# A two-layer perceiver on one core: projections on fp16 halves of fp32 values, with the lower halves of the turned tiles taken from PSUM by VectorE

## The reference, cut to what matters

```
kv = y_main @ [Wk, Wv] + bias             # context rows 256 wide, 2 x 512 columns
x  = x + attn(ln(q), ln(k), v) @ Wo + bo  # cross-attention
x  = x + selfattn(ln(x) @ Wq, ln(x) @ Wk, ln(x) @ Wv) @ Wo + bo
x  = x + ffn(x)
```

## Time and profile before

| | us |
|---|---|
| median of 3 runs | 3878.39 (3876.9 to 3882.73) |
| the profiled execution, its own time | 3881.73 |
| its span, first to last instruction | 3880.0 |
| context attention of layer 0, 16 batch elements | about 180 to 1338.6 |
| self-attention of layer 0 | 1338.6 to about 1590 |
| TensorE busy (matmul) / VectorE / ScalarE / GpSimd | 86% / 69% / 56% / 51% of the span |

### The profile page before, as it was taken

The page is one execution under the profiler, slowest core; times in us unless marked ns, Lnnn a source line. Parts: engine busy times, 40 slices in busy tenths (PEclk is TensorE's granted clock), DMA queues, the critical chain, the costliest instruction groups (busy, mean ns, idle before and its releaser), DMA issues. The chain is left out here.

```text
span 3880.0 us, 87607 instructions
## 1 busy us (share of the span) xinstructions
PE 3347.8 (86%) x34694; PEld 2418.0 (62%) x34694; DVE 2684.3 (69%) x4083; ACT 2172.2 (56%) x3767; POOL 1987.9 (51%) x2436
## 2 busy tenths in 40 slices
PE   5799999999999599548991589999999999959739
PEld 2577777777777455436770357777777777745425
DVE  5688888888888234336774478888888888816552
ACT  1367777777777422115660247777777777732231
POOL 5267767767767411232214527767767767731000
PEclk7899999999999699768995799999999999969869
DMA  2200000000000120008986110000000000030010
GB/s 78 72 29 28 29 28 21 28 30 20 29 29 11 60 51 0 32 15 285 300 269 190 23 65 28 29 25 25 29 29 20 28 30 20 11 85 0 22 65 22
DMA packets 98467, 212.45 MB, mean 55 GB/s; under 512 B 35669, under 2 KB 44629, under 8 KB 91946
## 3 DMA queue, kind: packets, MB, share of 16 engines
q1 hardware_dynamic: 89386, 181.98, 14.3%
q0 software_dynamic: 8704, 25.19, 2.3%
HBM read 174.58 MB, written 32.56 MB: 53 GB/s over the span
## 5 line engine op out<-in xcount | busy, mean ns | idle before, releaser
L265 POOL TENSOR_TENSOR a_elo<-a_e 128x1024 f16<-128x1024 f32 (+1 forms) x448 | 899.9, 2009 | 250.5 <-ACT a_e L337 241.3
L477 PE MATMUL a_ps_k<-l_wk,a_yh 128*128 128x512 f32 (+1 forms) x1664 | 625.4, 416 | 24.9 <-DVE a_yl L364 23.8
L477 PE MATMUL a_ps_v<-l_wv,a_yh 128*128 128x512 f32 (+1 forms) x1664 | 622.7, 415 | 13.7 <-DVE a_v L391 10.5
L335 ACT ACTIVATE a_e<-a_ps_t 128x1024 f32<-128x1024 f32 (+1 forms) x448 | 430.3, 961 | 143.9 <-PE a_ps_t L545 136.9
L400 DVE TENSOR_REDUCE a_mx<-a_ps_m 128x2 f32<-128x1024 f32 x384 | 466.2, 1214 | 6.8 <-PE a_ps_m L515 4.3
L246 POOL TENSOR_TENSOR a_khat<-a_kc,a_rstd 128x512 f32<-128x512 f32 (+1 forms) x416 | 449.6, 1088 | 17.5 <-PE a_ps_kt L498 7.0
L337 ACT ACTIVATE a_e<-a_ps_t 128x1024 f16<-128x1024 f32 (+1 forms) x448 | 427.5, 954 | 1.6 <-PE a_ps_o L572 1.6
L364 DVE TENSOR_TENSOR a_yl<-a_y,a_yh 128x256 fp32r<-128x256 f32 (+1 forms) x416 | 385.7, 928 | 22.4 <-ACT a_yh L293 18.5
L477 PEld LDWEIGHTS a_ps_k<-l_wk,a_yh 128*128 128x128 f32 (+1 forms) x1664 | 304.8, 183 | 143.4 <-issue 45.8
L477 PEld LDWEIGHTS a_ps_v<-l_wv,a_yh 128*128 128x128 f32 (+1 forms) x1664 | 304.2, 183 | 138.8 <-issue 57.6
L568 PE MATMUL a_ps_o<-a_v,a_e 128*128 128x65 f16 (+1 forms) x3328 | 360.0, 195 | 18.7 <-POOL a_elo L265 18.7
(11 more groups left out here) (312 smaller groups left out, 7045.8 us busy)
## 6 DMA issues: line engine op xcount, KB each, us to landing
f_e_w<-in_m_w SPq DMA_DIRECT2D x32, 1024.0 KB
a_y<-in_ctx SPq DMA_DIRECT2D x32, 817.0 KB
a_y<-in_ctx SPq DMA_DIRECT2D x32, 768.0 KB, 4.7
f_e_w<-in_m_w SPq DMA_DIRECT2D x32, 512.0 KB
eo_dram<-f_e_eo SPq DMA_DIRECT2D x32, 512.0 KB, 5.5
f_raw<-in_f_w SPq DMA_DIRECT2D x2, 2730.0 KB
qs_dram<-p_qc SPq DMA_DIRECT2D x32, 128.0 KB, 2.4
...
```

What stands on the lines that cost most here:

```text
L265: pool.tensor_tensor(elo[0:r, t, :, 0:w], e32[0:r, t, :, 0:w], e16[0:r, t, :, 0:w], ALU.subtract)\
L335: act.activation(e32[0:r, t, :, 0:w], ps_t[0:r, :, 0:w], ACT.Exp)
L477: m = pe.matmul(out[0:r, :], part[:, t, c, 0:r], w[:, wpart, c, :], start=(c == 0 and a == 0), stop=(c == KC - 1 and a == 2))
```

## The change

In the context attention the two parts of the context and of its weights become fp16 (upper part = rounded to fp16, lower part = the rest). The weights are multiplied by 32 (`WSCALE`) before they are split and the evictions multiply by 1/32. In the self-attention the four products with 512-wide weights do the same: the weights are split when they have landed (ScalarE `weight_high`, VectorE `weight_low`), the turned context output, the turned normalised x and the turned attention output are evicted as an upper part by ScalarE and a lower part by VectorE out of the same PSUM bank (`g_cl`, `f_xl`, `b_cl`), and each product is three sets of fp16 matmuls. In layer 0 q and k come out turned (weights stationary, x moving, 128 columns), so that their turns and bias adds by VectorE go; their biases come with the evictions (`qb` on VectorE, `kt` on ScalarE in four pieces). The output product moves to a slot of its own (`h_out`, one slot later); the loop is written out; loads and first waits are in another order.

```diff
-        yh = sb("yh", [P, 2, KC, P], F32R)
-        yl = sb("yl", [P, 2, KC, P], F32R)
+        yh = sb("yh", [P, 2, KC, P], F16)
+        yl = sb("yl", [P, 2, KC, P], F16)
...
-                                   ACT.Copy).then_inc(vh_done, 1)
+                                   ACT.Copy, scale=1.0 / WSCALE).then_inc(vh_done, 1)
...
-                    dve.tensor_tensor(yl[:, t, :, 0:r], y[:, :, i * P:i * P + r], yh[:, t, :, 0:r].bitcast(F32),
+                    dve.tensor_tensor(yl[:, t, :, 0:r], y[:, :, i * P:i * P + r], yh[:, t, :, 0:r],
                                       ALU.subtract).then_inc(yl_done, 1)
...
-                    dve.tensor_tensor(kc[0:r, kc_slot(at, i), :], ps_k[0:r, :], bk[0:r, :], ALU.add).then_inc(kc_done, 1)
+                    dve.scalar_tensor_tensor(out=kc[0:r, kc_slot(at, i), :], in0=ps_k[0:r, :], scalar=1.0 / WSCALE,
+                                             in1=bk[0:r, :], op0=ALU.mult, op1=ALU.add).then_inc(kc_done, 1)
...
-                    dve.tensor_tensor(v[0:r, at.nbp, i, :, 66:130], ps_v[0:r, :].rearrange("p (a d) -> p a d", d=64),
-                                      v[0:r, at.nbp, i, :, 0:64], ALU.subtract).then_inc(vl_done, 1)
+                    dve.scalar_tensor_tensor(out=v[0:r, at.nbp, i, :, 66:130],
+                                             in0=ps_v[0:r, :].rearrange("p (a d) -> p a d", d=64), scalar=1.0 / WSCALE,
+                                             in1=v[0:r, at.nbp, i, :, 0:64], op0=ALU.mult, op1=ALU.subtract)\
+                       .then_inc(vl_done, 1)
...
-                dve.tensor_copy(wk[:, 0], wkf).then_inc(g["hi_done"], 1)
-                dve.tensor_copy(wv[:, 0], wvf).then_inc(g["hi_done"], 1)
+                dve.tensor_scalar(wk[:, 0], wkf, WSCALE, None, ALU.mult).then_inc(g["hi_done"], 1)
+                dve.tensor_scalar(wv[:, 0], wvf, WSCALE, None, ALU.mult).then_inc(g["hi_done"], 1)
                 dve.wait_ge(g["hi_done"], 2)
-                dve.tensor_tensor(wk[:, 1], wkf, wk[:, 0].bitcast(F32), ALU.subtract)
-                dve.tensor_tensor(wv[:, 1], wvf, wv[:, 0].bitcast(F32), ALU.subtract)
+                dve.scalar_tensor_tensor(out=wk[:, 1], in0=wkf, scalar=WSCALE, in1=wk[:, 0], op0=ALU.mult,
+                                         op1=ALU.subtract)
+                dve.scalar_tensor_tensor(out=wv[:, 1], in0=wvf, scalar=WSCALE, in1=wv[:, 0], op0=ALU.mult,
+                                         op1=ALU.subtract)
                 dve.wait_ge(g["cb_in"], 16)
...
-                for n in range(2):
-                    load_x(n)
-                large = ["wo_x", "wq", "wk", "wv", "wo"]
-                for k in large[:1] + [k for k in loads if k not in large] + large[1:]:
-                    sp.dma_start(loads[k], raw[k]).then_inc(g[f"load_{k}"], 16)
+                load_x(0)
+                for k in ["wo_x"] + list(W) + [k for k in widths if k != "wo_x"]:
+                    if k != "cb_x":
+                        sp.dma_start(loads[k], raw[k]).then_inc(g[f"load_{k}"], 16)
+                    if k == "wo_x":
+                        load_x(1)
                 for n in range(2, TT):
...
+                def weight_high(*names):
+                    for k in names:
+                        act.wait_ge(g[f"load_{k}"], 16)
+                        act.activation(split[k][0][:, :, :].rearrange("p k n -> p (k n)"), loads[k], ACT.Copy, scale=WSCALE)\
+                            .then_inc(g[f"hi_{k}"], 1)
...
+                        for c in range(4):
+                            t = act.activation(kt[u][:, c, :], bank[u][3][:, c * P:(c + 1) * P], ACT.Identity,
+                                               bias=W["bk"][:, c:c + 1], scale=1.0 / WSCALE)
...
-                slots(act, f_xt, b_v, b_exp, b_pt, g_ct, b_ct, f_kt)
+                slots(f_xt, b_v, b_exp, b_pt, g_ct, f_kt, b_ct)
...
+                def f_xl(n, u):
+                    dve.wait_ge(g["xth"], n + 1)
+                    dve.tensor_tensor(xts[u][1][:, :, :], bank[u][0][:, :].rearrange("p (c n) -> p c n", c=4),
+                                      xts[u][0][:, :, :], ALU.subtract).then_inc(g["xt_done"], 1)
+                    if n == 0:
+                        weight_low("wq", "wk", "wv", "wo")
...
+                            t = dve.scalar_tensor_tensor(
+                                out=qb[u][:, :, :, a, :].rearrange("p g b q -> p (g b) q"),
+                                in0=bank[u][2][:, :].rearrange("p (j q) -> p j q", j=8), scalar=qmask[:, a:a + 1],
+                                in1=bqm[:, a, :, :].rearrange("p g b -> p (g b)").unsqueeze(2).broadcast_to([P, 8, 64]),
+                                op0=ALU.mult, op1=ALU.add)
...
+                def ctx_low(dst, hi, bank_, cb, done):
+                    src = bank_[:, :].rearrange("p (b g a q) -> p b g a q", b=2, g=2, a=2)
+                    for a in range(2):
+                        for h in range(2):
+                            d = dst[:, a, h, :].rearrange("p (b q) -> p b q", b=2)
+                            c = cb[:, 2 * a + h:2 * a + h + 1] if cb is not None else 0.0
+                            t = dve.scalar_tensor_tensor(out=d, in0=src[:, :, h, a, :], scalar=c,
+                                                         in1=hi[:, a, h, :].rearrange("p (b q) -> p b q", b=2),
+                                                         op0=ALU.add, op1=ALU.subtract)
+                    t.then_inc(done, 1)
...
-                slots(dve, f_xn, b_softmax, b_ls, b_rl, f_q, f_k, b_o, f_qb, g_res, g_stat, g_aggr, b_x)
...
+                if rope:
+                    slots(b_sm0, f_xn, b_sm1, f_xl, h_x, b_ls, b_rl, f_q, f_k, g_cl, b_o, f_qb, b_cl, g_res, g_stat, g_aggr)
+                else:
+                    slots(f_xn, b_sm0, b_sm1, f_xl, h_x, b_ls, b_rl, f_qb, g_cl, b_o, b_cl, g_res, g_stat, g_aggr)
...
+                PARTS = ((0, 0), (0, 1), (1, 0))
...
+                def out_product(n, c, hi, lo, w, out, done):
+                    weights(n, w)
+                    pe.wait_ge(g[hi], n + 1)
+                    for i, (a, b) in enumerate(PARTS):
+                        if a:
+                            pe.wait_ge(g[lo], n + 1)
+                        for k in range(4):
+                            t = pe.matmul(out[:, :], c[a][:, k // 2, k % 2, :], split[w][b][:, k, :],
+                                          start=(i == 0 and k == 0), stop=(i == 2 and k == 3))
+                    t.then_inc(g[done], 1)
...
+                def turned_projection(n, u, w, out, chunks):
+                    weights(n, w)
+                    pe.wait_ge(g["xt_done"], n + 1)
+                    for c in chunks:
+                        for i, (a, b) in enumerate(PARTS):
+                            for k in range(4):
+                                t = pe.matmul(out[:, c * P:(c + 1) * P], split[w][b][:, k, c * P:(c + 1) * P],
+                                              xts[u][a][:, k, :], start=(i == 0 and k == 0), stop=(i == 2 and k == 3))
+                    return t
...
-                slots(pe, b_sc, b_va, f_tr2, b_vb, f_q, b_tr5, f_k, b_pv, f_tr3, g_tr1, f_tr4, b_tr6, g_out, b_out)
...
+                if rope:
+                    slots(b_sc, b_va, h_out, f_tr2, b_vb, f_q, b_tr5, f_ka, g_tr1, b_pv, f_tr3, f_tr4, b_tr6, g_out)
+                else:
+                    slots(b_sc, b_va, h_out, f_tr2, b_vb, f_q, b_tr5, f_ka, g_tr1, b_pv, f_kb, b_tr6, g_out)
```

More of the change, by code:

```diff
@@ L1155, in b_ct, with weight_low @@
                     act.wait_ge(g["tr6"], n + 1)
-                    ctx_evac(ct[u], bank[u][0], W.get("cb"), g["ct2"])
+                    if n >= 2:
+                        act.wait_ge(g["y2"], n - 1)
+                    ctx_evac(cts[u][0], bank[u][0], W.get("cb"), g["cth"])
+                weight_high("wo_x")
                 if not rope:
                     act.wait_ge(g["load_cb"], 16)
-                slots(act, f_xt, b_v, b_exp, b_pt, g_ct, b_ct, f_kt)
+                slots(f_xt, b_v, b_exp, b_pt, g_ct, f_kt, b_ct)
             @block.vector
             def _(dve):
-                for k in ("sink", "cos", "sin") if rope else ("bq", "bk"):
+                def weight_low(*names):
+                    for k in names:
+                        dve.wait_ge(g[f"hi_{k}"], 1)
+                        dve.scalar_tensor_tensor(out=split[k][1][:, :, :].rearrange("p k n -> p (k n)"), in0=loads[k],
+                                                 scalar=WSCALE, in1=split[k][0][:, :, :].rearrange("p k n -> p (k n)"),
+                                                 op0=ALU.mult, op1=ALU.subtract).then_inc(g[f"lo_{k}"], 1)
+                weight_low("wo_x")
+                for k in ("sink", "cos", "sin") if rope else ("bq",):
                     dve.wait_ge(g[f"load_{k}"], 16)
@@ new lines, in f_qb @@
+                        for a in range(2):
+                            t = dve.tensor_scalar(qb[u][:, :, :, a, :], bank[u][0][:, :].rearrange(
```

(40 more changed lines are left out.)

232 lines of the change are left out of this document (134 added, 98 removed).

## The result

The changed kernel takes 3721.7 us in the median (3721.48 to 3722.07) against 3877.64 for the kernel before in the same session: a ratio of 0.9597, 95% interval 0.958 to 0.9614. The profiled execution has a span of 3719.8 us, 160.2 less than before. Predicted were 3753 us and 125 less.

What follows compares the result with a forecast made beforehand. TensorE was taken to bind except in the context period's second part, where VectorE does; 70 + 31 + 16 + 8 = 125 us off the profiled 3881.73 gave 3756.7, 3753 as a median, range 3690 to 3810.

Steps and rivals of the forecast that it cites:

- A product of the context attention: Context attention, TensorE: six 512-column matmuls in fp16 instead of fp32r take 1.29 us instead of 1.515.
- The first part of the period: Context attention, the 45.0 us where TensorE binds: 2.3 us offered per batch element, 1.9 taken.
- The second part: Context attention, the 26.8 us where VectorE is full: 0.3 us gained per batch element, of 0.66 free.
- rival 1: Context attention: TensorE binds throughout; if VectorE's waits for GpSimd in `y_low` shrink, the whole 150 us comes, 3673; chance 0.13.
- the context term of 70: Context attention: 2.2 us gained per batch element, 70 us over 32, bounds 16 to 150.
- Layer 0, a slot of 20.6 us: Self-attention of layer 0: each slot falls from 25.1 to 20.6 us, 31 us over 7 slots (5 to 37).
- rival 3: Self-attention, layer 0: turned q and k cost 0.08 or 0.11 us per matmul, not 0.055: 3770 or 3790; chance 0.10.
- Layer 1, a slot of 20.3 us: Self-attention of layer 1: each slot falls from 22.6 to 20.3 us, 16 us over 7 slots (0 to 21).
- both waits of rows 10 stay: Self-attention of layer 1: TensorE's two waits for VectorE per slot, 0.89 and 0.98 us, remain.
- Start and end, 4 us per layer: Start and end of each self-attention, weight splitting and closing chain included: 4 us gained per layer, 8 in all.
- 5 (`y_low` and `p_low` meet more often): Context attention: `y_low` on VectorE waits more often for GpSimd's `p_low`, a loss of 15 us, 3893; chance 0.05.

Runs made afterwards that it cites:

- more_pe_loose: The changed kernel with one repeated 512-column matmul ahead of each of k8 to k12, where TensorE was busy all the time: 3754.44 us, ratio 0.9664.
- more_pe_tight: The changed kernel with one repeated 512-column matmul ahead of each of k1 to k5, where VectorE was at 98%: 3739.73 us, ratio 0.9628.

## Why the prediction came out as it did

The sign, the range (3690 to 3810) and the place of most of the gain were right; the point, 3753, was 31 us too high, and 3721.7 lies 3 us outside the narrower 3725 to 3785 that the forecast itself was given. Term by term the profiled gain is 125 + 33 (context) - 2 (slots of layer 0) - 13 (slots of layer 1) + 20 (starts and ends), less some 3 us by which 32 whole periods overstate the context: three errors of over 10 us, of which the sum shows only the balance. By its own steps:

- **A product of the context attention**, 1.515 to 1.29 us: right. The distances make 1.09 + 0.215 = 1.31, and `k_centred`, now with the scale in it, takes 683 ns in the mean where it took 682.
- **The first part of the period**: 2.3 us offered, 1.9 taken because ScalarE and GpSimd would stand at 90%. They do stand at 38.47 and 38.70 of 42.94 us, just as computed, and it cost nothing: the measured 2.41 is the whole offer, and `more_pe_loose` shows TensorE alone binding there. Term too small by 0.5 x 32 = 16 us.
- **The second part**: "I take 0.3 us of the 0.66 free". It gave 0.81. The reading that VectorE binds it was right, for both kernels, as `y_low` on GpSimd showed (0.83 and 0.77 us). What failed is "None of its instructions gets shorter". Its six `y_low` there went from a mean of 1055 to 1001 ns, 0.3 us together (one from 1.09 to 0.97 us, one from 0.97 to 0.75), which is the way that rival 1 named. The rest is VectorE's idle time: its wait for `v_high` went from 0.39 to 0.20, and two gaps, ahead of a maximum and of a `k_centred`, closed by 0.12 and 0.15. `more_pe_tight` lengthened both `y_low` and opened both gaps again, but not the wait. Another 0.5 x 32 = 16 us. These two steps are the missing 33 us of the context term of 70.
- **Layer 0, a slot of 20.6 us**: 20.27. Turned q and k cost what was taken, not what rival 3 had. TensorE's timeline of one slot:

```profile
1369.14 2.84 PE L1427 MATMUL s_bank<-s_xt,s_wq 128*128 128x128 f16 x48
...
1378.67 0.66 PE L1387 MATMUL s_bank<-ident,s_o 128*128 128x128 f32 x4 [0.65 <-DVE s_o L1325]
```

  48 matmuls in 2.84 us, the last one's way of 0.2 in it, are 0.055 each. The rule of the Trainium skill ("TensorE: Matmul & The Clock Gate", "Back-to-back issue gap"), 81 ns per matmul of 128 columns, would make it 3.9 us, an estimate; the measurement decides against it here. The wait before the turn of o is 0.65 us and not the 1.14 that the slot was computed with; that is more than the whole difference of 0.33. The seven slots gave 28.7 of 31 us: the first two gained 2.0 and 2.5 us and not 4.8. In the first, TensorE waits for VectorE to split the q weight, 4.89 us in layer 0 and 4.81 in layer 1, where it had waited 0.78 before:

```profile
1311.93 4.41 PE L1427 MATMUL s_bank<-s_xt,s_wq 128*128 128x128 f16 x48 [4.89 <-DVE s_wq L1194]
...
3332.89 4.24 PE L1416 MATMUL s_bank<-s_wq,s_xt 128*128 128x512 f16 x12 [4.81 <-DVE s_wq L1194]
```

  The prediction had seen this splitting and counted it into the start; in layer 1 it makes the first slot 2 us longer than it was, 24.3 us against 22.3.
- **Layer 1, a slot of 20.3 us**: 20.8 where the clock is full. The step that failed is "both waits of rows 10 stay". The one for k, 0.89 us, is gone; one of 1.06 for `xn` is new; and the one for o goes from 0.98 to 2.02, as `g_cl` stands ahead of it. The waits grow by 1.2 us, and 19.6 + 1.2 is the measured 20.8. The text priced VectorE's new passes by their sum and not by what is queued behind them, though it did so in layer 0. And the slots aren't alike, as these windows of the changed kernel show:

```profile
3385.80:3406.50 20.70, 17.24 (x154) 11.47 (x152) 18.53 (x42) 5.75 (x14) 3.65 (x4) 1.00 0.00 1
...
3427.30:3450.20 22.90, 19.43 (x155) 12.29 (x153) 19.04 (x43) 5.75 (x14) 3.65 (x4) 0.89 0.00 1
3450.20:3473.90 23.70, 20.25 (x153) 12.48 (x152) 18.54 (x42) 5.75 (x14) 3.64 (x4) 0.86 0.00 1
```

  Only three of seven ran at a granted clock of 1.00. In the last slot the fall comes with the wait for o:

```profile
3449.27 1.12 PE L1387 MATMUL s_bank<-ident,s_o 128*128 128x128 f32 x4 [2.02 <-DVE s_o L1325]
3450.18 5.33 PE L1381 MATMUL s_bank<-s_wo_x,s_cx 128*128 128x512 f16 x12
```

  The product takes 5.33 us and not 2.75, and from 3450.2 to 3455.2 the granted clock is 0.50, the 1.2 GHz level. So the seven gave 3.1 us instead of 16: 20.8 in place of 20.3 accounts for some 3.5 of the 13 us, the two slots at 0.89 and 0.86 for 5, and the first two slots, late and below the full clock, for the rest.
- **Start and end, 4 us per layer**: the starts gave 5.0 and 2.9 us, just the 8 taken. The ends gave 10.4 and 10.2 more, which were not counted at all: behind the start of the eighth output product come two more slots of work with the same shortened products. The text multiplied a slot's gain by the seven distances it could see. Against the 4 taken, starts and ends gave 11 us more in layer 0 and 9 more in layer 1, which hid the 13 missing from the slots of layer 1. That these errors nearly cancel was luck, and so was the exactness of the starts, given how such starts vary.
- **Rivals.** 1 (TensorE binds throughout) was partly so: the gain lies between forecast and rival, two `y_low` of the tight stretch did shrink, and TensorE alone did not bind there. 5 (`y_low` and `p_low` meet more often) went the other way, 928 to 843 ns in the mean of all of the kernel's; `more_pe_loose` shows the meeting can come back with 1.08 us of TensorE work, and that it costs nothing where TensorE binds. The rows of the kernel before did not show which way such a drift would go.

Not settled: why 0.63 of 1.08 us arrives in the tight stretch and not more or less, and why the granted clock falls after one wait of 2.02 us in layer 1 and not after the next.

## What to carry to other kernels

Take the gain of a shorter operation per stretch between the same two instructions, and where one engine is at 97% test it by moving some of its work away: 0.8 us per period was to be had before the change and after it, beside a TensorE shown as 98% busy before. For a software pipeline, multiply a slot's gain by the tiles, not by the distances between them: the work behind the last start shrinks as well. When passes are added to an engine, ask for each waiting product what now stands ahead of its releaser; putting `b_o` ahead of `g_cl` is a one-word edit and gave 1.0 us per slot in layer 1.
